# Prologue of a LayerNorm, linear-attention and mixture-of-experts kernel: the low half of x formed in PSUM by a negative identity and copied out by ScalarE, and the normalization dealt out anew

## What is computed

```python
x = L0_attn_x                                   # (16, 512, 128) f32
xn = _layernorm(x, axis=-1)
s = attention(xn, ...)                          # 16 heads of 8, chunked scan
g = silu(0.5 * shared(xn) + 0.5 * routed(xn))   # 8 experts, top 2 by softmax(xn @ gate_W.T)
return x + s * g
# _layernorm: (x - mean) / sqrt(var + 1e-5)
```

## Time and profile before

| | |
|---|---|
| median of 3 runs | 737.22 us (736.26 to 739.5) |
| profiled execution | 739.27 us |
| its span, first to last instruction | 737.5 us |
| granted TensorE clock, mean | 0.981 |
| busy in the span | PE 90%, DVE 78%, ACT 66%, POOL 62% |

### The profile page before, as it was taken

One profiled execution on the slowest core, in us unless ns is written; L12 is line 12 of the kernel. 1 busy time (PEld: TensorE's weight loads), 2 busy tenths in 40 slices (PEclk: granted clock), 3 DMA queues, 4 the chain that ended last, 5 costly groups with the idle time before them and its releaser, 6 DMA issues.

```text
span 737.5 us, 22308 instructions
## 1 busy us (share of the span) xinstructions
PE 661.2 (90%) x8520; PEld 459.4 (62%) x8520; DVE 576.4 (78%) x1095; ACT 485.2 (66%) x985; POOL 455.1 (62%) x490
## 2 busy tenths in 40 slices
PE   2677798896999999999999999999996998999993
PEld 1444465564665666566666667788894676667672
DVE  6989987987676887667766666677664799999996
ACT  5855578764666666566666666666665677877772
POOL 2435322225777777777777777677776566666663
PEclk9999999999999999999999999999999999999997
DMA  9931111111111233433333334333455567766742
GB/s 240 279 101 44 44 58 45 44 44 34 46 44 51 94 102 108 136 105 109 107 104 109 97 101 147 102 104 107 93 105 156 169 215 215 221 217 190 221 136 58
DMA packets 88616, 86.75 MB, mean 118 GB/s; under 512 B 11394, under 2 KB 65284, under 8 KB 88516
## 3 DMA queue, kind: packets, MB, share of 16 engines
q1 hardware_dynamic: 79428, 66.70, 28.9%
q0 software_dynamic: 9088, 18.63, 9.8%
HBM read 50.82 MB, written 34.47 MB: 116 GB/s over the span
## 4 chain that ended last, share of the span: by engine, by line
PE 51%; DVE 29%; issue 7%; ACT 7%; DMA 3%; POOL 2%; SPq 0%; DVEq 0%; ACTq 0%; POOLq 0%
PE banks L1512 9%; PE banks L1514 8%; PE banks L1513 8%; DVE wwords L1262 6%; DVE hidden L1279 6%; PE banks L1552 6%; DVE hidden L1177 5%; PE banks L1533 4%; PE banks L1532 4%; PE banks L1531 4%; ACT hidden L750 2%; PE banks L1463 2%; ACT hidden L746 2%; DVE ffn L945 2%; DMA srows<-normed_rows,source 1%
## 5 line engine op out<-in xcount | busy, mean ns | idle before, releaser
L750 ACT CAST hidden<-hidden 128x512 f16<-128x512 f32 x206 | 127.2, 618 | 144.0 <-DVE hidden L1177 143.7
L1181 DVE TENSOR_TENSOR hidden<-hidden 128x512 f16<-128x512 f32 x178 | 123.2, 692 | 82.5 <-ACT hidden L750 82.1
L622 POOL DMA_INDIRECT srows<-normed_rows,source x142 | 148.5, 1046 | 55.7 <-issue 40.2
L1177 DVE TENSOR_TENSOR hidden<-hidden,banks 128x512 f32<-128x512 f32 x206 | 140.9, 684 | 41.1 <-ACT hidden L746 35.6
L1531 PE MATMUL banks<-wwords,hidden 128*128 (+1 forms) x824 | 149.6, 220 | 1.4 <-DVE hidden L1181 1.0
L1533 PE MATMUL banks<-wwords,hidden 128*128 (+1 forms) x824 | 149.5, 220 | 0.0
L1532 PE MATMUL banks<-wwords,hidden 128*128 (+1 forms) x824 | 149.5, 220 | 0.0
L746 ACT ACTIVATE hidden<-banks 128x512 f32<-128x512 f32 x206 | 122.8, 596 | 29.9 <-PE banks L1514 29.4
L1512 PE MATMUL banks<-sx,wwords 128*128 128x512 f16 (+1 forms) x368 | 121.5, 330 | 2.0 <-DVE wwords L967 1.3
L1514 PE MATMUL banks<-sx,wwords 128*128 128x512 f16 (+1 forms) x368 | 121.6, 330 | 0.0
L1513 PE MATMUL banks<-sx,wwords 128*128 128x512 f16 (+1 forms) x368 | 121.5, 330 | 0.0
(11 more groups left out here) (213 smaller groups left out, 1423.0 us busy)
## 6 DMA issues: line engine op xcount, KB each, us to landing
rows<-x SPq DMA_DIRECT2D x32, 256.0 KB, 5.3
rows<-expert_rows SPq DMA_DIRECT2D x32, 256.0 KB, 3.4
normed_rows<-rows SPq DMA_DIRECT2D x16, 256.0 KB, 3.9
r_rows<-rows SPq DMA_DIRECT2D x16, 256.0 KB, 2.1
rd_rows<-rows SPq DMA_DIRECT2D x16, 256.0 KB, 2.1
stage<-r_rows SPq DMA_DIRECT2D x16, 256.0 KB, 5.7
k_rows<-rows SPq DMA_DIRECT2D x16, 256.0 KB, 2.0
kd_rows<-rows SPq DMA_DIRECT2D x16, 256.0 KB, 2.1
```

Source lines behind the costliest of these rows:

```text
L622: G.indirect_dma_start(srows[:, q % NXB, t, :], None, rows_in, bass.IndirectOffsetOnAxis(source[:, at:at + 1], 0)).then_inc(sem[f"s_in{q % ...
L750: A.copy(guh[:, i % 4, :], gu[:, i % 2, :]).then_inc(sem["gu_hi"], 1)
L1177: V.tensor_tensor(gu[:, i % 2, :], sg[:, i % 2, :], psum[2 * (i % 2) + 1][:, :], ALU.mult).then_inc(sem["gated"], 1)
L1181: V.tensor_tensor(gul[:, i % 4, :], gu[:, i % 2, :], guh[:, i % 4, :], ALU.subtract).then_inc(sem["gu_lo"], 1)
```

## The change

It touches the prologue alone.

- **Low half.** After the transposes of a batch the bank holds x. PE then adds minus the identity times `xh` to the same bank (`pe_rest`, one 128x512 f16 matmul), so that the bank holds x minus its high half, and ACT copies that to f16 `xl` (`act_rest`). DVE's subtraction `dve_flip` is gone. The negative identity `minus_one` is made by one ACT instruction and lies in `f2`, which is free until the end of the expert steps. The transposes are written as matmuls with `is_transpose=True` and one accumulation group for the bank.
- **Normalization.** Of the four tiles of a batch POOL does three. The first tile is ACT's in even batches and DVE's in odd ones. Readers of a normalized batch wait through `normed`.
- **Decay tables.** The 128x1024 product goes from DVE to POOL (`pool_gaps`).
- **Order.** DVE takes the statistics of batch 0 ahead of its small constants, and its three weight splits and `dve_r_weights` behind the loop. ACT's three weight splits start at turn 14 instead of 10. PE does no `pe_up(0)` inside the loop; it comes after the last gate matmuls, and needs `xl` of all batches.

```diff
+        def normed(engine, b):
+            engine.wait_ge(sem["normed_a"], b // 2 + 1)
+            engine.wait_ge(sem["normed_v"], (b + 1) // 2)
+            engine.wait_ge(sem["normed_g"], (b + 1) * (TPS - 1))
...
+            def pool_gaps():
+                G.wait_ge(sem["const_in"], 16)
+                G.wait_ge(sem["rates"], 4)
+                G.tensor_tensor(wtmp[:, :, :], rep(rates[:, :], Q), rep_mid(C("gap"), HEADS), ALU.mult).then_inc(sem["gaps"], 1)
+
             def pool_norm(b):
                 G.wait_ge(sem["shift"], b + 1)
-                for t in range(b * TPS + TPS // 2, (b + 1) * TPS):
+                for t in range(b * TPS + 1, (b + 1) * TPS):
...
+            def act_norm(b):
+                A.wait_ge(sem["shift"], b + 1)
+                t = b * TPS
+                A.activation(rows[:, t, :], rows[:, t, :], ACT.Identity, bias=shift[:, t:t + 1],
+                             scale=rstd[:, t:t + 1]).then_inc(sem["normed_a"], 1)
+
+            def act_rest(b):
+                A.wait_ge(sem["x_rest"], b + 1)
+                A.copy(xl[:, b * XS + 2:(b + 1) * XS], psum[b % 4][:, :]).then_inc(sem["x_lo"], 1)
+
+            def act_minus_one():
+                A.wait_ge(sem["const_in"], 16)
+                A.mul(minus_one[:, :], C("ident"), -1.0).then_inc(sem["minus_one"], 1)
...
-            for b in range(nb + 3):
+            for b in range(nb + 4):
                 if b < nb:
                     act_std(b)
-                if 1 <= b <= nb:
+                if 1 <= b < nb and b % 2 == 1:
                     act_norm(b - 1)
-                if 2 <= b < nb + 2:
-                    act_flip(b - 2)
-                if 10 <= b < 13:
-                    act_split_w(0, b - 10)
+                if 3 <= b < nb + 3:
+                    act_flip(b - 3)
+                if b >= 4:
+                    act_rest(b - 4)
+                if FIRST_SPLIT <= b < FIRST_SPLIT + 3:
+                    act_split_w(0, b - FIRST_SPLIT)
...
+                if b % 2 == 1:
+                    t = b * TPS
+                    V.wait_ge(sem["shift"], b + 1)
+                    V.tensor_scalar(rows[:, t, :], rows[:, t, :], rstd[:, t:t + 1], shift[:, t:t + 1],
+                                    ALU.mult, ALU.add).then_inc(sem["normed_v"], 1)
...
+            dve_stats(0)
             dve_prologue()
             dve_rates()
-            for b in range(nb + 3):
+            for b in range(1, nb + 1):
                 if b < nb:
                     dve_stats(b)
-                if 1 <= b <= nb:
-                    dve_norm(b - 1)
-                if b >= 3:
-                    dve_flip(b - 3)
-                if 11 <= b < 14:
-                    dve_split_w(0, b - 11)
-                if b >= nb + 1:
-                    dve_r_weights(b - nb - 1)
+                dve_norm(b - 1)
+            for part in range(3):
+                dve_split_w(0, part)
+            dve_r_weights(0)
+            dve_r_weights(1)
...
+            def pe_rest(b):
+                if b == 0:
+                    T.wait_ge(sem["minus_one"], 1)
+                T.wait_ge(sem["x_hi"], b + 1)
+                T.matmul(psum[b % 4][:, :], minus_one[:, :], xh[:, b * XS + 2:(b + 1) * XS], start=False, stop=True,
+                         skip_group_check=True).then_inc(sem["x_rest"], 1)
...
-            for b in range(nb + 3):
-                if 2 <= b < nb + 2:
-                    pe_flip(b - 2)
-                if b == nb + 1:
-                    pe_up(0)
-                if b >= 3:
-                    pe_gate(b - 3)
+            for b in range(nb + 2):
+                if b < nb:
+                    pe_flip(b)
+                if 1 <= b <= nb:
+                    pe_rest(b - 1)
+                if b >= 2:
+                    pe_gate(b - 2)
```

More of the change, by code:

```diff
@@ L238, in build @@
         f2y = sb("f2y", [P, P], F16)
+        minus_one = f2
         take = carve(rows[:, :, :].rearrange("p a b -> p (a b)"))
@@ L393, in build @@
         LOWS_FIRST = 12
+        FIRST_SPLIT = 14
+        def normed(engine, b):
+            engine.wait_ge(sem["normed_a"], b // 2 + 1)
+            engine.wait_ge(sem["normed_v"], (b + 1) // 2)
+            engine.wait_ge(sem["normed_g"], (b + 1) * (TPS - 1))
         ROUTE_CHOSEN = 12
@@ L466, in sp_normed @@
             def sp_normed(b):
-                nc.sync.wait_ge(sem["normed_a"], (b + 1) * TPS // 2)
-                nc.sync.wait_ge(sem["normed_g"], (b + 1) * TPS // 2)
+                normed(nc.sync, b)
                 nc.sync.dma_start(rows_in[b * SEQ:(b + 1) * SEQ, :].rearrange("(t p) d -> p t d", p=P),
@@ L602, in pool_prologue @@
                         G.memset(t[:, b * XS:b * XS + 2], 0.0).then_inc(sem["zero_cols"], 1)
+            def pool_gaps():
+                G.wait_ge(sem["const_in"], 16)
+                G.wait_ge(sem["rates"], 4)
+                G.tensor_tensor(wtmp[:, :, :], rep(rates[:, :], Q), rep_mid(C("gap"), HEADS), ALU.mult).then_inc(sem["gaps"], 1)
             def pool_norm(b):
                 G.wait_ge(sem["shift"], b + 1)
-                for t in range(b * TPS + TPS // 2, (b + 1) * TPS):
+                for t in range(b * TPS + 1, (b + 1) * TPS):
                     G.tensor_scalar(rows[:, t, :], rows[:, t, :], rstd[:, t:t + 1], shift[:, t:t + 1],
-                                         ALU.mult, ALU.add).then_inc(sem["normed_g"], 1)
+                                    ALU.mult, ALU.add).then_inc(sem["normed_g"], 1)
             def pool_first_low(i):
@@ L679, in pool_program @@
             pool_prologue()
+            pool_gaps()
             for b in range(nb):
@@ L711, in act_std @@
                 A.activation(std[:, T4], mv[:, T4, 1], ACT.Sqrt, bias=C("eps")).then_inc(sem["std"], 1)
[L713 to L717, removed]
             def act_flip(b):
@@ L794, in act_decays @@
             def act_decays():
-                A.wait_ge(sem["const_in"], 16)
-                A.wait_ge(sem["rates"], 6)
+                A.wait_ge(sem["rates"], 5)
+                A.wait_ge(sem["gaps"], 1)
                 A.activation(wmat[:, :, :], wtmp[:, :, :], ACT.Exp, scale=-1.0).then_inc(sem["decays"], 1)
@@ L844, in act_program @@
             act_rates()
+            act_minus_one()
             act_decays()
-            for b in range(nb + 3):
+            for b in range(nb + 4):
                 if b < nb:
                     act_std(b)
-                if 1 <= b <= nb:
+                if 1 <= b < nb and b % 2 == 1:
                     act_norm(b - 1)
-                if 2 <= b < nb + 2:
-                    act_flip(b - 2)
-                if 10 <= b < 13:
-                    act_split_w(0, b - 10)
+                if 3 <= b < nb + 3:
[4 more added lines that the diff above has]
+                    act_split_w(0, b - FIRST_SPLIT)
             for i in range(NS + LAG):
@@ L920, in dve_rates @@
                 V.tensor_scalar(rates[:, :], rates[:, :], 200.0, None, ALU.min).then_inc(sem["rates"], 1)
-                V.wait_ge(sem["rates"], 4)
-                V.tensor_tensor(wtmp[:, :, :], rep(rates[:, :], Q), rep_mid(C("gap"), HEADS), ALU.mult).then_inc(sem["rates"], 1)
+                V.wait_ge(sem["rates"], 3)
                 V.tensor_scalar(nrate[:, :], rate[:, :], -1.0, None, ALU.mult).then_inc(sem["rates"], 1)
@@ L1422, in pe_flip @@
                     T.wait_ge(sem["const_in"], 16)
-                T.wait_ge(sem["normed_a"], (b + 1) * TPS // 2)
-                T.wait_ge(sem["normed_g"], (b + 1) * TPS // 2)
+                normed(T, b)
                 for t in range(TPS):
-                    i = T.transpose(psum[b % 4][:, t * P:(t + 1) * P], rows[:, b * TPS + t, :], C("ident"))
+                    i = T.matmul(psum[b % 4][:, t * P:(t + 1) * P], rows[:, b * TPS + t, :], C("ident"), start=(t == 0), stop=(t == TPS - 1),
+                                 is_transpose=True)
                 i.then_inc(sem["flipped"], 1)
+            def pe_rest(b):
[4 more added lines that the diff above has]
+                         skip_group_check=True).then_inc(sem["x_rest"], 1)
             def pe_gate(b):
@@ L1676, in pe_out_last @@
                 k.then_inc(sem["out_last"], 1)
-            for b in range(nb + 3):
-                if 2 <= b < nb + 2:
-                    pe_flip(b - 2)
-                if b == nb + 1:
-                    pe_up(0)
-                if b >= 3:
-                    pe_gate(b - 3)
+            for b in range(nb + 2):
[5 more added lines that the diff above has]
+                    pe_gate(b - 2)
             for i in range(NS + LAG):
                 if i < NS:
-                    if i > 0:
-                        pe_up(i)
+                    pe_up(i)
                     if i == ROUTE_AT:
```

6 lines of the change are left out of this document (removed).

## The result

| | before | after |
|---|---|---|
| median, same chip | 736.75 us (734.03 to 741.69, 16 runs) | 731.47 us (728.6 to 735.11, 16 runs) |
| profiled execution / span | 739.27 / 737.5 us | 729.46 / 727.2 us |
| granted TensorE clock, mean | 0.981 | 0.976 |

The ratio is 0.9933 with a 95% interval of 0.9915 to 0.995, so 3.7 to 6.3 us faster; the medians are 5.3 apart.

A forecast was written before the change was run, and what follows sets the result against it. DVE was taken to bound the prologue. Loop -5.8 us (later start included), loop's end +2.6, tail +0.8 gave -2.4, from the 737.22 us median to 734.8; range 732.4 to 737.6.

The forecast's parts named there:

- product on POOL: Start of the loop: the 128x1024 product, moved from DVE, takes 2.3 us on POOL, between 1.23 and 3.0.
- shift 0: End of batch 0's statistics and shift on DVE: comes at 12.25 us instead of 11.06, 1.2 later.
- shift 0 to shift 14: Prologue loop at DVE's pace, 1.6 instead of 2.06 us a batch: 22.2 us plus 0.3 for collisions with POOL.
- shift 14: Batch 14's shift on DVE, near the loop's end: at 34.7 us against 40.47, 5.8 us gained gross.
- POOL's last tile done: End of the loop: batch 15's last normalized tile ready at 39.4 us, 4.7 behind shift 14 instead of 2.1.
- last tile to mark: Tail, from the last transposes through `pe_up(0)` and silu to the first expert product: 7.0 us instead of 6.2.
- mark: Start of DVE's first expert product, L1177 in the kernel before: at 46.4 us instead of 48.79.
- the gain at the mark is not lost behind it: Experts behind the mark: DVE has no idle time, so the gain carries through; rival, no gain, 737.2 us, chance 0.10.
- The rival that POOL becomes the bound: Prologue normalization: tiles take 0.71 us instead of 0.44, POOL needs 2.1 us a batch, time 742.0; chance 0.06.
- the array stays at its lower level in the prologue: PE in the prologue: stays at 1.2 GHz, a 128x512 matmul starting every 0.43 us, `pe_up(0)` taking 2.57.
- My rival: PE's added matmuls raise the array to 2.4 GHz earlier: 4.1 us gained in all, 733.1 us; chance 0.12.
- PE paces it: Prologue loop: PE needs 1.81 us a turn, or copies get into its way, time 735.9 us; chance 0.18.

The follow-up runs named there:

- again: The changed kernel once more, with no edit: 734.5 us against 737.29 for the kernel before, ratio 0.9939.

## Why the prediction was right and wrong

| step | forecast | `again`, with `pe_up(0)` at 2.4 GHz |
|---|---|---|
| product on POOL | 2.3 us | 1.90 |
| shift 0 | 12.25 | 11.70 |
| shift 0 to shift 14 | 22.45 | 23.03 |
| shift 14 | 34.7 | 34.73 |
| POOL's last tile done | 39.4 | 38.53 |
| last tile to mark | 7.0 | 4.96 (6.25 with `pe_up(0)` at 1.2 GHz) |
| mark | 46.4 | 43.49 (44.78) |

**Right**: what bounds the kernel (DVE in the prologue), that the gain at the mark is not lost behind it (0.4 to 1.8 us come on top), and that the subtraction L958 leaves DVE's path for an addition on PE and ACT that lies beside it. Taking the subtraction back brings the mark to 52.80. Shift 14 fell on the forecast, by luck, from two errors that cancel: the start was 0.55 us earlier than forecast and the pace 0.6 slower, 3.29 us for two batches instead of 3.2. The rival that POOL becomes the bound is out: its tiles took about 0.45, not 0.71.

**The step that failed** is "the array stays at its lower level in the prologue". I had it as a rival, with the right mechanism and a chance of 0.12, and argued against it that PE had been 75% busy with transposes and gate and had not risen, "and a quarter of a turn is all that comes in". That quarter was decisive, as the kernel before with one more matmul a turn shows. The tail term of 7.0 us was thereby mis-sized: `pe_up(0)` took 1.29 instead of 2.57, the transposes 0.63 instead of 1.09, the new matmul 0.38 instead of 0.63, together 2.0 of the 2.9 us that the mark came too early. My rival had priced 1.7 for it and left out that the transposes gain too (0.46). It also gave for the granted clock of 1.00 in the prologue; these are rows of 50 to 60 us, but from 12 to 44 it reads 1.00 as well. The Trainium skill's rule (TensorE: Matmul & The Clock Gate, Part 4: PE-mode transpose), that transposes don't count as activity for the clock gate, agrees with the kernel before and with the one with L984 on DVE, where transposes and 128x8 matmuls alone never raised it. I had read it as a reason for the level to stay; it was a reason to ask what the new matmul, which is no transpose, would do.

**Sizes**: the other 0.9 us is the end of POOL's work. I took 2.6 us for six tiles, three splits at 0.54 each and 0.2 for DVE's tile, 4.5 in all; it was 3.53. DVE's tile cost nearly nothing (2.59 with it), and the splits 0.94. ACT, whose splits begin at turn 14, hands DVE its high halves one by one, so that the third split comes when POOL is all but done. I had read the splits' order from the code, and not what each waits for. The rule of an exclusive lock between DVE and POOL (the Trainium skill, SBUF — State Buffer, section SBUF: two separate sides) agrees in direction with 2.59, 3.53 and 4.14 us for six tiles with no, two and three splits beside them; by these numbers a split of 0.60 us costs POOL about 0.5, not its whole length.

**The rival "PE paces it"** was not borne out. Its premise was 1.04 us from the transposes to the new matmul; at the lower level it was 0.88 where nothing was waited for (16.71 to 17.59). PE's turn there took 1.67 us (16.71 to 18.38), as the forecast's 1.65 has it. The next took 1.94, but in it the transposes are over at 19.26 and the new matmul starts at 19.50, behind ACT's copy. At the upper level PE waits 0.64 us in every other turn. Whether PE's 1.67 at the lower level would have held up DVE's 1.65 over the whole loop no run shows; an estimate from these two numbers is 0.3 us over 13 turns.

**Not explained**: why the gain of the first pair grows from 4 to 7 us between the 43rd and the 103rd product and settles at 5.8, and why the level fell ahead of `pe_up(0)` in one of the four traces of the changed kernel. That costs 1.3 us at the mark.

## What to carry to other kernels

When a change adds even one wide matmul a turn to a stretch of transposes and narrow matmuls, price the stretch at both clock levels, transposes included, and don't take the level that the stretch had without it as given. Subtracting by a negative identity in PSUM takes 0.60 us a batch off VectorE where that sets the pace, but it turns one VectorE operation into a second copy on ScalarE: without moving other work off ScalarE the bound only changes its place (no gain with two tiles on ACT). Before moving DVE work that slows POOL, see what spaces it now; earlier is not cheaper (0.6 us lost when the splits became free to run together).

## What was unexpected in the hardware

- f32 transposes gain from the upper level too: four of 128x128 take 0.63 us instead of 1.09.
- The granted clock shows the level only once it has changed. Before the first rise it reads 1.00 although four transposes take 1.09 us (12 to 44 us in before; 12 to 20 us in the changed kernel). After a fall it reads 0.50: 32 to 44 us in the kernel with two tiles on ACT, and 0.51 in the one with the added matmul in before, against 1.00 from 19.2 to 25.4 us, while its level is up. So a 1.00 at the start of a kernel has to be checked against the time between starts.
- POOL took 1.90 us for a 128x1024 f32 product for which DVE takes 1.23. Half of that size, with f16 out, takes it 1.16, so doubling it overstated.
- One chip took 843 us for the kernel that the others do in 737 to 738. Its prologue agrees to 0.1 us. The kernel before with the added matmul is not behind before at the 48th expert product (177 us); from there the loss grows steadily, to 107 us at the 205th. The cause was not tried.
